# A mixed attention kernel: one weight split moved up, a DMA order changed, and 112 masked maxima replaced by plain reductions

## What is computed

```
xn  = layernorm(x)
# branch 1: local attention, 16 query heads, 4 key/value heads of 32
q, k, v = xn Wq' + bq, xn Wk' + bk, xn Wv' + bv
q, k = rope(rmsnorm(q) * qn_w), rope(rmsnorm(k) * kn_w)
A   = softmax(mask(q k' * scale))      # key j <= query i, i - j <= 64
y1  = (A v) Wo' + bo
# branch 2: routed attention, 16 query heads, one shared key and value
g   = softmax(xn W_gate')              # 16 heads; t = argmax, p = max
fq, fk, fv = split(xn W_qkv')
k_s, v_s = head t of fk, p * head t of fv
y2  = softmax(causal(fq k_s' / sqrt(32))) v_s
out = x + y1 + y2
```

## Time and profile before

| | us |
|---|---|
| median of 3 runs | 674.92 (674.49 to 675.19) |
| the profiled execution, device time | 676.8 |
| its span | 675.6 |
| TensorE (PE) busy | 641.0 |
| VectorE (DVE) busy | 459.9 |
| ScalarE (ACT) busy | 362.5 |
| GpSimd (POOL) busy | 444.0 |

### The profile page before, as it was taken

One profiled execution on the slowest core, in us unless ns is written; L12 is line 12 of the kernel. 1 busy time (PEld: TensorE's weight loads), 2 busy tenths in 40 slices (PEclk: granted clock), 3 DMA queues, 4 the chain that ended last, 5 costly groups with the idle time before them and its releaser, 6 DMA issues.

```text
span 675.6 us, 19434 instructions
## 1 busy us (share of the span) xinstructions
PE 641.0 (95%) x7432; PEld 509.3 (75%) x7432; DVE 459.9 (68%) x1296; ACT 362.5 (54%) x906; POOL 444.0 (66%) x384
## 2 busy tenths in 40 slices
PE   3888999999999999999999899999999999999997
PEld 2667788888788887888788677777777777777775
DVE  3847657658567665756665389887878787879454
ACT  4446554526453445445256555656565566656684
POOL 3856875386755649472896357776878687868730
PEclk9998999999999999999999899999999999999999
DMA  8623213231322142212216631502214131402011
GB/s 299 209 58 107 57 48 114 76 93 56 91 69 79 35 118 89 75 54 76 64 33 161 165 96 57 136 26 80 82 51 112 51 110 36 104 28 88 4 34 33
DMA packets 64942, 56.63 MB, mean 84 GB/s; under 512 B 6480, under 2 KB 48848, under 8 KB 64848
## 3 DMA queue, kind: packets, MB, share of 16 engines
q1 hardware_dynamic: 62704, 54.45, 27.2%
q10 hardware_dynamic: 2144, 0.93, 0.5%
HBM read 37.20 MB, written 17.89 MB: 82 GB/s over the span
## 4 chain that ended last, share of the span: by engine, by line
PE 86%; DVE 4%; POOL 3%; DMA 2%; issue 2%; ACT 2%; ACTq 1%; DVEq 0%; POOLq 0%
PE gemm L942 20%; PE s_ps L1051 12%; PE od_ps L1100 11%; PE st_ps L1084 10%; PE gemm L1028 7%; PE gemm L938 6%; PE od_ps L1114 5%; PE win L1002 4%; PE win L987 3%; PE s_ps L1123 2%; PE av L1014 2%; DMA rope_t<-rope 2%; PE av L1041 1%; PE tp L953 1%; PE tp L909 1%
## 5 line engine op out<-in xcount | busy, mean ns | idle before, releaser
L942 PE MATMUL gemm<-w_tok,xt 128*128 128x512 f32 (+1 forms) x768 | 185.9, 383 | 1.8 <-ACT xt L1410 0.8
L942 PEld LDWEIGHTS gemm<-w_tok,xt 128*128 128x128 f32 x768 | 131.1, 194 | 25.1 <-issue 1.2
L1317 DVE CUSTOM_DVE_ANT_0 s_ps<-s_ps,x_ln 128x512 f32<-128x512 f32 (+3 forms) x224 | 127.3, 618 | 25.1 <-PE s_ps L1051 24.8
L1051 PE MATMUL s_ps<-k_stack,w_tok 96*128 96x512 f32 (+2 forms) x336 | 101.2, 384 | 0.3 <-DVE x_res L1282 0.3
L1084 PE MATMUL st_ps<-w_tok,k_stack 98*128 98x512 f32 x288 | 99.2, 413 | 0.2 <-ACT p_loc L1538 0.2
L1538 ACT ACTIVATE p_loc<-st_ps 128x512 f32<-128x512 f32 x144 | 77.7, 598 | 36.1 <-PE st_ps L1084 35.0
L1490 ACT ACTIVATE p_loc<-win,l_max 128x96 f32<-128x96 f32 x256 | 61.1, 392 | 32.6 <-DVE l_max L1256 32.6
L1051 PEld LDWEIGHTS s_ps<-k_stack,w_tok 96*128 96x128 f32 x336 | 55.1, 188 | 27.8 <-DVE picked_fk L1317 12.3
L1659 POOL TENSOR_TENSOR p_loc<-p_loc,l_rec 128x1536 f32<-128x1536 f32 x16 | 44.1, 2759 | 36.6 <-DVE l_rec L1268 36.6
L1635 POOL TENSOR_TENSOR rope_b<-qkv,sin_t 128x128 f32<-128x128 f32 (+1 forms) x32 | 27.4, 878 | 62.0 <-DVE qkv L1234 61.8
L1538 ACT ACTIVATE p_loc_t<-st_ps 128x512 f32<-128x512 f32 x96 | 52.4, 599 | 19.4 <-PE st_ps L1084 18.9
(11 more groups left out here) (171 smaller groups left out, 1264.1 us busy)
## 6 DMA issues: line engine op xcount, KB each, us to landing
w_tok<-q_parts SPq DMA_DIRECT2D x72, 128.0 KB, 2.6
q_parts<-qt SPq DMA_DIRECT2D x120, 64.0 KB
x_ln<-x SPq DMA_DIRECT2D x8, 512.0 KB, 4.6
x_res<-x SPq DMA_DIRECT2D x16, 256.0 KB, 2.8
partial<-x_res SPq DMA_DIRECT2D x16, 256.0 KB, 2.3
w_tok<-partial SPq DMA_DIRECT2D x8, 512.0 KB, 5.1
raw<-w_tok SPq DMA_DIRECT2D x3, 1024.0 KB, 13.7
v_win<-v_rows SPq DMA_DIRECT2D x64, 48.0 KB, 2.2
```

The costliest lines, as they stand in the source:

```text
L942: i = e.matmul(g[:, 0:cols], xs[l][:, k, a * P:(a + 1) * P], w_tok_p[r][:, k, c0:c0 + cols], start=first, stop=last)
L1051: e.matmul(s_ps[bank][:, 0:cols], q_op[b][0:HALVES, i, h, :], k_stack[0:HALVES, b * S + c0:b * S + c0 + cols], start=True, stop=True).then ...
L1317: e.tensor_tensor_reduce(out=s[:, 0:cols], in0=s[:, 0:cols], in1=causal[:, S - width + c0:S - width + c0 + cols], scale=1.0, scalar=dst if ...
```

## The change

Three edits. The split of the last piece (wo) is no longer issued where the planner finds it due, but by the normalisation of round 1, right behind `x_factors`; the planner's own account of engine time stays as it was, so nothing else in its list moves. In ScalarE's queue the rope table is loaded second, ahead of rank and bias, and the norm weights and the scale last. In the routed phase a piece that ends short of the row's width, which is an unmasked one, is reduced straight from its bank, without the mask, the nop and the accumulator's read.

```diff
@@ -207,8 +207,9 @@
     def make_pieces(upto):
         while pieces_made[0] <= min(upto, len(PIECES) - 1):
             n = pieces_made[0]
-            do("w_hi", n)
-            do("w_lo", n)
+            if n < len(PIECES) - 1:
+                do("w_hi", n)
+                do("w_lo", n)
             piece_ready[n] = p.busy(p.now, ("A", 1.9), ("V", 2.3)) + HOP
@@ -228,6 +229,9 @@
         do("x_factors", n)
         if n == 0:
             do("tables")
+        if n == 1:
+            do("w_hi", len(PIECES) - 1)
+            do("w_lo", len(PIECES) - 1)
         yield 0, [("V", 0.7), ("G", 1.0)]
@@ -1313,6 +1317,9 @@
                 if c0:
                     lane.wait_ge(*M["rs_max"].of((u, t - HQ)))
+                if c0 + cols < width:
+                    e.tensor_reduce(dst, s[:, 0:cols], AX.X, ALU.max).then_inc(*M["rs_max"].did((u, t)))
+                    continue
                 e.nop(nofuse=True)
@@ -1373,12 +1380,12 @@
         e.dma_start(idt[:, :], ident).then_inc(*M["ident_in"].did("all", inc=16))
+        e.dma_start(rope_t[:, :, :, :], rope.rearrange("(t p) a d -> p t a d", p=P)).then_inc(
+            *M["rope_in"].did(inc=16))
         for dst, src in ((rank_t, rank), (bias, b_qkv)):
             e.dma_start(dst[:, :], src.to_broadcast(dst.shape)).then_inc(*M["bias_in"].did("all", inc=16))
         for dst, src in ((norm_w[:, :, :, :].rearrange("p a b d -> p (a b d)"), w_norm), (scale_t[:, :], scale)):
-            e.dma_start(dst, src.to_broadcast(dst.shape)).then_inc(*M["rope_in"].did(inc=16))
-        e.dma_start(rope_t[:, :, :, :], rope.rearrange("(t p) a d -> p t a d", p=P)).then_inc(
-            *M["rope_in"].did("all", inc=16))
+            e.dma_start(dst, src.to_broadcast(dst.shape)).then_inc(*M["rope_in"].did("all", inc=16))
```

## The result

| | us | ratio to the kernel before, 95% interval |
|---|---|---|
| before, median of its runs beside the changed kernel | 675.06 (674.33 to 677.52) | |
| changed, median of 6 runs | 669.29 (667.88 to 671.48) | 0.9915 [0.9894, 0.9937] |
| changed, 6 more runs (e11; before beside it: 676.01) | 668.38 (668.05 to 670.54) | 0.9896 [0.9873, 0.9918] |

The profiled executions differ by 6.1 us in span (675.6 and 669.5). Their own device times are 676.8 and 671.4.

What follows compares the result with a forecast made beforehand. The prediction took the ramp's GpSimd rope chain and VectorE's subtraction, plus short routed waits for score banks, as bounds. Terms -0.4 + 0 - 1.3 = -1.7 us gave 673.2 us from a median of 674.92; range 670.0 to 675.9.

Steps and rivals of the forecast that it cites:

- What bounds the kernel: Whole kernel: TensorE is 95% busy, so only the ramp (0 to about 54 us) and short routed waits can gain.
- Part 2: Ramp, rope table loaded second: the tables' last load still lands at 18.5 us; 0, between -0.7 and +1.0 us.
- lower bound of -0.7: Ramp, earlier table loads: at most 0.7 us gained, since the rope products need the biased q at 24.68.
- Part 1: Ramp, moved split: the subtraction starts first and holds GpSimd's L1619, 2.0 us late, leaving a gain of 0.4 us.
- rival B: Ramp, no collision: L1619 goes ahead of the moved subtraction, the split gains 2.4 us, total 671.2 us; chance 0.25.
- Part 1's second term: Ramp, after the split moves: picked_fk waits for matmuls ending at 45.9, running 2.4 us earlier if the place is free.
- Part 3: Routed phase: 112 maxima become plain reductions, freeing banks 0.1 us earlier; 16 weight-load waits gain 0.08 each, 1.3 us.
- upper bound of 3.8: Routed maxima: the most gained, 16 waits of 4.6 us in all less 16 x 0.05 of ordinary gap.
- Rival C: Ramp: TensorE's idle stretch grows to 4.2 us and the clock falls behind it, costing 1.7; up to 675.8 us; chance 0.15.

Runs made afterwards that it cites:

- e11: The changed kernel itself run again, 6 more runs beside the kernel before (676.01 us): 668.38 us, ratio 0.9896.
- e1: Only the load order changed (rope table second in ScalarE's queue, norm weights and scale last), against the kernel before: 673.25 us, ratio 0.9964.
- e2: Only the split of the last piece moved behind round 1's layernorm factors, against the kernel before: 674.53 us, ratio 0.9983.
- e4: Load order and moved split together, maxima as before, against the kernel before: 670.98 us, ratio 0.9937.
- e3: Only the 112 unmasked maxima made plain reductions, against the kernel before: 673.64 us, ratio 0.9974.
- e5: e2 plus a wait: the last piece's subtraction waits for GpSimd's last rope product of tile (0, 0); 671.43 us, 0.9947 against the kernel before.
- e8: Changed kernel with rank and bias loaded ahead of the rope table, norm weights and scale behind it: 671.83 us in two groups, 0.9945 against the kernel before.
- e10: e8 plus the wait of e6: 668.19 us over 4 runs, 0.9887 against the kernel before.
- e6: Changed kernel plus a wait: the last piece's subtraction waits for GpSimd's second layernorm factor of round 1; 668.82 us, 0.9911 against the kernel before.
- e7: Changed kernel with norm weights and scale loaded right behind the rope table, rank and bias last: 667.97 us, 0.9899 against the kernel before.
- e9: Changed kernel with the load order of e7 and the wait of e6: 667.37 us over 4 runs, 0.9873 against the kernel before.

## Why the prediction was wrong

**What bounds the kernel** was right: the ramp's rope chain and VectorE's 3.18 us subtraction, and the short waits in the maxima. The whole gain is in these places: 4.2 us in the ramp, forecast 0.4, and 1.9 in the maxima, forecast 1.3.

**Part 2 failed**, and with it the sum. The step was "the last of them, now the scale, I put at the same 18.5", costed at 0. It lands at 16.3, and the other queue's weights come 1.2 us sooner too. I had named the sign of it ("I am wrong altogether if L1594 moves by more than half a microsecond"): it moved by 2.3, and went ahead of the subtraction that used to hold it. The earlier loads alone are worth 1.8 us at the milestone (e1, with one clock fall more than before), though there L1594 is still held. The lower bound of -0.7 took the biased q at 24.68 as fixed, whereas the weights moved too. In the changed kernel q is there at 24.37 and the first sine product starts at 24.44 for 25.52 before, 1.1 earlier; L1626 keeps it, 35.64 for 36.83.

**Part 1, the collision, was right about the kernel that it described**: with the old load order (e2) the hold is there, with 1.8 us on L1623 for the 2.0 forecast. But in the full change it doesn't happen. R moves the last rope product from 36.83 to 35.64 (35.19 in e4), while the subtraction doesn't start before ScalarE's copy and VectorE's factors are done: 36.61 in e4. That this is the 36.60 of the forecast is luck, since e2, the kernel that the forecast described, has 35.78. What parts the two engines is one more hold, at 27 us, which the prediction didn't look at. The subtraction of piece 4 (the qt weights) and GpSimd's cosine products meet there, in e2 (old load order) and in the changed kernel:

```profile
26.61 2.29 DVE L1142 TENSOR_TENSOR w_qt<-raw,w_qt 128x2048 fp32r<-128x2048 f32 x1 [0.90 <-ACT w_qt L1395]
26.72 3.73 POOL L1645 TENSOR_TENSOR qkv<-qkv,cos_t 128x128 f32<-128x128 f32 x2
```

```profile
26.32 1.72 POOL L1648 TENSOR_TENSOR qkv<-qkv,cos_t 128x128 f32<-128x128 f32 x2
26.98 3.20 DVE L1142 TENSOR_TENSOR w_qt<-raw,w_qt 128x2048 fp32r<-128x2048 f32 x1 [0.90 <-ACT w_qt L1398]
...
28.11 3.47 POOL L1652 TENSOR_TENSOR qkv<-qkv,rope_b 128x640 f32<-128x640 f32 x1
```

With the old order GpSimd has waited for the sine table and comes 0.1 us too late. Where the tables are ready first, it waits only for q, gets both cosine products in, and it is VectorE that is put off by 0.9 us. From the biased q to the last rope product it is then 11.95 us in place of 12.8, and to the subtraction of piece 5, without a clock fall, 13.37 (e4) in place of 12.46 (e2): GpSimd, second by 0.36, becomes first by 1.42. The old order at 27 us stands in before, e2, e3, e5, e8, e10 and also e6; the new one in e1, e4, e7, e9, e11 and the changed kernel. In the changed kernel it comes as late as 38.67 for a second reason, a clock fall that slows the chunk ahead of ScalarE's copy (3.01 us before). From its timeline and windows:

```profile
31.79 4.63 PE L942 MATMUL gemm<-xt,w_qt 128*128 128x256 f32 x24 [2.81 <-DVE g_exp L1188]
```

```profile
30.00:34.00 4.00, 2.21 (x14) 2.21 (x15) 3.93 (x12) 0.31 (x2) 3.83 (x3) 0.84 0.07 20
34.00:38.00 4.00, 4.00 (x22) 3.67 (x22) 1.74 (x8) 2.14 (x4) 2.96 (x3) 0.73 0.12 36
```

The statement against rival B, that tables, subtractions and rope products "move together", is what failed: earlier landings change which of two neighbours goes first, at 16.4 us and, what counts, at 27.

**Part 1's second term was mis-sized.** "picked_fk then waits for its matmuls, which end at 45.9" took the wrong product. In e2 and e5 picked_fk starts before or with the three matmuls that I had assigned to it; what it needs is the product whose last three matmuls start, in the kernel before, at 42.57 and end at 43.5. Unhindered it can start behind x_t, at 44.2 (43.48 with 0.69), so the move is worth about 4.2 us and not 2.4, if no one is held. e5 shows it: picked_fk at 44.63, 3.8 earlier, and the milestone 4.0 earlier. With the hold, 48.38 became 46.79 and not 47.95, in spite of a clock fall. Rival B's 671.2 carried the same wrong 2.4; with 4.0 and the measured maxima it would have read 674.92 - 4.0 - 1.9 = 669.0, beside 669.29. That they lie so close is partly luck, as this sum has nothing for the earlier loads: between e5 and e4 they are worth 0.7 us by the ratios, and between the traces of e5 and the changed kernel 0.2 at the milestone (1.1 in e11's, whose milestone is at 70.54). The mechanism of the result is thus rival B's, brought about by part 2, at nearly twice B's price for the ramp.

**Part 3 was right in kind and too small.** Groups by form of the changed kernel, then what waited for VectorE at the score matmuls, of the changed kernel and of before (a line gives the time and the number of waits):

```profile
L1321 DVE TENSOR_REDUCE picked_fk<-s_ps 128x1 f32<-128x512 f32 x112 | 72.3, 684 | 9.0 <-PE s_ps L1055 8.9
```

```profile
L1055 PE MATMUL s_ps<-k_stack,w_tok x336: 274/392/507, 386.3 to 624.1; 96*128 96x512 f32 x84, 96*128 96x256 f32 x56, 96*128 96x384 f32 x28
...
  DVE picked_fk L1324: 5.5, 24
  DVE picked_fk L1321: 4.4, 21
```

```profile
L1051 PE MATMUL s_ps<-k_stack,w_tok x336: 274/392/507, 390.5 to 630.2; 96*128 96x512 f32 x84, 96*128 96x256 f32 x56, 96*128 96x384 f32 x28
...
  DVE picked_fk L1317: 12.3, 51
```

112 reductions of 0.684 (forecast 0.68). The weight loads' waits for VectorE fall from 12.3 to 9.9 us, 2.4, and the phase from 239.7 to 237.8 us, 1.9, against the forecast 1.3. I priced each of the 16 waits at the 0.1 us by which its bank comes free sooner. Those of 0.35 did become 0.25, but those of 0.23 to 0.29 came down to the 0.20 or less that many of these loads show anyway, or went altogether: only six of the 16, all of 0.25, are left above that, and 45 waits in place of 51. The saving comes to what lies between my 1.3 and the upper bound of 3.8.

**The clock.** Rival C's fall to half speed is real, about 3.4 us long, and *not tied to one place*. Windows of before around the end of phase 1, and of e4 over the first of them:

```profile
375.00:380.00 5.00, 3.47 (x41) 2.64 (x39) 1.67 (x4) 0.98 (x2) 3.99 (x2) 0.81 0.67 175
380.00:385.00 5.00, 5.00 (x33) 3.73 (x35) 0.69 (x1) 2.33 (x5) 0.00 (x0) 0.85 0.97 244
```

```profile
375.00:380.00 5.00, 5.00 (x57) 3.81 (x56) 0.69 (x1) 3.34 (x7) 0.83 (x2) 1.00 1.00 255
```

Between two milestones of that stretch before takes 9.72 us with a fall (376.85 to 386.57), and e1 8.16 without (375.20 to 383.36): a fall costs 1.6 us. In the ramp it came at 54 to 57 us before, at 40 to 43 in e2, 32 to 35 in e5, 32 to 36 in the changed kernel, 30 to 34 in e7, e8, e10 and e11, twice in e1 (31 to 34 and 51 to 55), and not at all in e4, e6 and e9. The length of the idle stretch ahead of it doesn't decide it alone: the chunk near 31 us starts behind 2.81 us of idle in the changed kernel and 2.80 in e4, and behind 1.88 in e5 and 1.91 in e2, and only the first of each pair has a fall there. Such falls are likely part of why runs of one kernel spread (3.6 us in the changed kernel, 6.0 in e2), and one can decide a race of two engines (e8). The two profiled executions of before and after both hold one fall in the ramp and one near 375, so their difference of 6.1 us has little of it.

**What stays open.** Why the queue drains later when the rope table is its last load: its place is shown to matter, no experiment separates the causes (the packets' size and the sharing with SyncE's queue would be the candidates). Landings also vary by up to about 1 us between executions of like orders, so what e7 gains over the changed kernel (0.9899 against 0.9915 and 0.9896) is not settled; and e9's 1.0 us isn't divided between the order and the wait. The slower executions of e2 (12 runs from 671.93 to 677.93) weren't traced apart from the one at 675.03.

## What to carry to other kernels

Where two engines hold each other out, ask of every edit upstream which of the two will be first afterwards; a margin of 0.2 us is no forecast, and a semaphore wait that fixes the order can be worth more than the move itself (here 2.4 us, by the ratios, against 1.1). Don't take the time at which a queue empties as fixed when its order changes: look at both queues' landings, and at what they release. Before you say what a step will wait for next, check in the trace that its operand really is the product you name, best by an instruction of the same kind that starts before that product.

## What the runs showed of the hardware that was not expected

- The hold strikes the smallest operations. A GpSimd power over 128x2 took 0.70 us alone and 2.68 to 2.83 when VectorE's 2.29 us subtraction had started up to 0.2 us before it (e4, e8 against e10). The Trainium skill (SBUF — State Buffer, Who interferes with whom) says that the shared port pair is an exclusive lock, held for the whole instruction. The traces agree for these products and subtractions, but not for GpSimd's long power: in e2 the subtraction starts at 35.78 under a power recorded to 36.00 and takes 2.29, and in the kernel before VectorE's 128x2 factor operation takes 0.17 under the power (35.27), where it takes 1.06 under a rope product in e4 (35.41).
- Adding one wait, and nothing else, took 674.53 to 671.43 (ratios 0.9983 and 0.9947).
- Moving one 256 KB load from last to second in its queue made the queue's last load land at 15.5 to 16.7 us in five traces, against 17.8 to 18.9 in four, and the copy of weights that come in another engine's queue start at 13.8 to 14.9, against 15.3 to 16.0.
- Falls of the clock to 1.2 GHz (granted 0.50), about 3.4 us long and worth 1.6 us, appear in different places of the ramp from one profiled kernel to the next, twice in e1, and nowhere in e4, e6 and e9. By delaying the copy of the last weights such a fall also decides which of VectorE and GpSimd comes first.
